# Expert up products: three float32r passes over fixed weight halves, or one full float32 product over weights copied for each slot

## The reference, cut to what matters

```python
# layer 1: gated, no shared expert
g, u = jnp.split(x @ gup.T, 2, axis=-1)              # gup: 1024 x 128 of one expert
acc = acc + ce[:, None] * (jax.nn.silu(g) * u @ dn.T)   # dn: 128 x 512

# layer 2: one up product per expert, and one shared expert for all tokens
shared = jnp.einsum('th,hd->td', jax.nn.silu(x @ shared_w1.T), shared_w2.T)
h = jnp.einsum('td,ehd->teh', x_flat, experts_w1)
expert_out = jnp.einsum('teh,edh->ted', jax.nn.silu(h), experts_w2)
```

## Time and profile before

| what | value |
|---|---|
| median of 3 runs | 3575.4 us (3574.93 to 3579.01) |
| the profiled execution's own time | 3567.43 us |
| its span, first to last instruction | 3565.3 us |
| mean granted TensorE clock | 0.931 of full speed |
| busy: TensorE, VectorE, ScalarE, GpSimd | 3055.0, 2421.9, 2133.5, 1222.4 us |
| first gather to last scatter, layer 2, first run | 2370.83 to 2567.51 us |

### The profile page before, as it was taken

One profiled execution on the slowest core, in us unless ns is written; L12 is line 12 of the kernel. 1 busy time (PEld: TensorE's weight loads), 2 busy tenths in 40 slices (PEclk: granted clock), 3 DMA queues, 4 the chain that ended last, 5 costly groups with the idle time before them and its releaser, 6 DMA issues. The chain is left out here.

```text
span 3565.3 us, 61688 instructions
## 1 busy us (share of the span) xinstructions
PE 3055.0 (86%) x20359; PEld 1919.6 (54%) x20359; DVE 2421.9 (68%) x6667; ACT 2133.5 (60%) x3201; POOL 1222.4 (34%) x1338
## 2 busy tenths in 40 slices
PE   4669999786658967999999779689778987998999
PEld 3533333344447852222222368668756875886787
DVE  7778988576964458999999454454586455656565
ACT  4448989664534545999999735433434344653564
POOL 4454551121546642010010276466536660001000
PEclk9879999998878988999999979899999998999999
DMA  1053440000021122010000321221202122000100
GB/s 58 1 165 112 126 130 18 1 1 24 0 118 40 48 86 89 21 30 21 21 30 2 132 72 48 79 106 46 82 7 93 46 75 80 1 1 10 59 10 12
DMA packets 87166, 187.15 MB, mean 52 GB/s; under 512 B 23169, under 2 KB 41409, under 8 KB 83793
## 3 DMA queue, kind: packets, MB, share of 16 engines
q1 hardware_dynamic: 60048, 117.66, 9.8%
q0 software_dynamic: 26816, 65.58, 5.9%
HBM read 121.23 MB, written 61.34 MB: 51 GB/s over the span
## 5 line engine op out<-in xcount | busy, mean ns | idle before, releaser
L2598 ACT ACTIVATE core_pr<-core_two 128x1024 f32<-128x1024 f32 (+3 forms) x896 | 787.5, 934 | 49.5 <-PE core_two L2565 45.8
L2634 DVE TENSOR_REDUCE core_mx<-core_one 128x1 f32<-128x512 f32 x778 | 491.4, 683 | 20.9 <-PE core_one L2517 13.7
L2577 PE MATMUL core_ps_o<-core_pr,core_vals 128*32 128x512 f32 (+3 forms) x3584 | 434.1, 559 | 1.7 <-ACT core_oT L2609 1.5
L2517 PE MATMUL core_one<-arena,queries 64*128 64x512 bf16 (+3 forms) x1472 | 375.3, 363 | 29.2 <-PEq L62 19.0
L2565 PE MATMUL core_two<-queries,arena 64*128 64x512 bf16 (+3 forms) x1792 | 341.4, 360 | 9.5 <-ACT core_pr L2598 6.8
L2517 PEld LDWEIGHTS core_one<-arena,queries 64*128 64x128 bf16 x1472 | 113.2, 94 | 297.0 <-DVE core_mx L2634 132.2
L2451 POOL COPY core_vals<-arena 128x288 f32<-128x288 f32 x32 | 14.7, 459 | 690.4 <-PE core_ps_o L2577 690.4
L2628 DVE CUSTOM_DVE_ANT_0 core_junk<-core_one,core_over 128x512 bf16<-128x512 f32 (+4 forms) x334 | 201.7, 644 | 26.3 <-PE core_one L2517 21.9
L2565 PEld LDWEIGHTS core_two<-queries,arena 64*128 64x128 bf16 x1792 | 94.3, 94 | 201.7 <-ACT core_pr L2598 145.4
L2604 ACT ACTIVATE core_over<-core_two 128x1024 f32<-128x1024 f32 (+4 forms) x167 | 159.9, 958 | 58.3 <-PE core_two L2540 45.6
L110 DVE CAST moe_second_x_hi<-moe_second_bank 128x128 fp32r<-128x128 f32 x142 | 41.4, 292 | 217.6 <-PE moe_second_bank L573 217.6
(11 more groups left out here) (656 smaller groups left out, 8030.2 us busy)
## 6 DMA issues: line engine op xcount, KB each, us to landing
arena<-expert_out SPq DMA_DIRECT2D x64, 256.0 KB, 3.6
expert_rows<-arena SPq DMA_DIRECT2D x13, 512.0 KB, 8.1
core_w_raw<-in_m_up POOLq DMA_DIRECT2D x25, 256.0 KB, 3.3
m_hi<-core_w_hi POOLq DMA_DIRECT2D x25, 256.0 KB, 2.4
m_lo<-core_w_lo POOLq DMA_DIRECT2D x25, 256.0 KB, 3.0
q_parts<-qkv_parts SPq DMA_DIRECT2D x16, 384.0 KB, 2.6
k_parts<-qkv_parts SPq DMA_DIRECT2D x16, 384.0 KB, 3.4
queries<-q_parts SPq DMA_DIRECT2D x64, 96.0 KB
```

Source lines behind the costliest of these rows:

```text
L2517: pe.matmul(one[bank[e]][:, 0:width], q_sb[rows, hq, pair, qt * P:(qt + 1) * P], k_sb[rows, hq, pair, kc * CW:kc * CW + width], start=True ...
L2577: mm = pe.matmul(ps_o[h * 32:(h + 1) * 32, off:CW], vals[:, hq % 2, j, h, :], pr[:, (n * N2 + k) % KEPT, h // 2, h % 2, off:CW], start=(j ...
L2598: a.activation(pr[:, step % KEPT, i, :, off:CW], two[spot[e] % 2][:, :, off:CW], ACT.Exp, scale=HD ** -0.5).then_inc(s_wide, 1)
L2634: v.tensor_reduce(at, scores, AX.X, ALU.max).then_inc(s_read, 1)
```

## The change

- The up product is a full float32 product with the weights standing and the rows moving: four matmuls of 128x128 for each half of 512, eight for a gated slot, four for a shared one. The result comes out turned, so that `turn_h`, `copy_h` and the tile `h` go; ScalarE's Silu or VectorE's multiply writes `hT` directly, which has 4 places (`HT`) where it had 2.
- [...] VectorE reads the slot's `woff` into a register and copies that expert's 128x512 (gated: 2 x 128x512) from `w_up` to `chosen`, two places in turn. Instead of two instructions that cut the rows it makes one plain copy of them (`copy_x`).
- `psY` has two banks instead of one.
- The float32r halves of the up weights of layers 1 and 2 are no longer made in `core0`, and each sparse stage loads the weights themselves, half as many bytes.
- Shared stages: `gathers_behind` is that of the gated stages, 8 gathers in front and one behind each scatter. The units run on every third round (`EVERY`). CHOOSING is 2 instead of 1. The transposes of chunks 2 and 3 come behind PLACING, those of chunks 4 to 7 into the table rounds 1, 2, 5 and 6; ScalarE normalises groups 2 and 3 behind the first units, group 3 in pieces within the table rounds.

```diff
-    up_hi, up_lo = (st.sb(f"up_{n}", [P, halves * W]) for n in ("hi", "lo"))
+    w_up = st.sb("w_up", [P, halves * W])
...
+    HT = 4
-    fetched = [gathers_behind(s, gated) for s in range(-1, SLOTS)]
+    fetched = [gathers_behind(s) for s in range(-1, SLOTS)]
...
-    CHOOSING, PLACING, ASIDE, BEHIND = (1, 3, 1, 2) if shared else (0, 0, 0, 0)
-    AT = 4
+    CHOOSING, PLACING, ASIDE, BEHIND = (2, 3, 1, 2) if shared else (0, 0, 0, 0)
+    AT, EVERY = 4, 3
+    TURNED_AT = (1, 2, 5, 6)
+    ADDED = {7: 3, 19: 4, 31: 5, 43: 6, 52: 7}
...
             def up(s):
-                pe.wait_ge(s_xlo, s + 1)
+                pe.wait_ge(s_xc, s + 1)
+                pe.wait_ge(s_wc, s + 1)
                 if s >= 2:
                     pe.wait_ge(s_h, s - 1)
                 for half, out in ((0, A), (1, B))[:halves]:
-                    mm = product(pe, out[s % 2][:], (x_hi[:, s % 2, :], x_lo[:, s % 2, :]),
-                                 [t[:, half * W:(half + 1) * W][:, bass.ds(at[s], HID)] for t in (up_hi, up_lo)])
+                    for j in range(4):
+                        mm = pe.matmul(out[s % 2][:, j * P:(j + 1) * P], chosen[:, s % 2, half, j * P:(j + 1) * P],
+                                       xrT[:, s % 2, :], start=True, stop=True)
                     mm.then_inc(s_up if half == halves - 1 else s_gate, 1)
...
-                if 1 <= s <= SLOTS:
-                    turn_h(s - 1)
-                always(1)
+                if s % EVERY == 0:
+                    always(1)
                 if s >= 2:
                     down(s - 2)
...
+            def choose_w(s):
+                e = v.value_load(woff[0:1, s:s + 1], min_val=0, max_val=7 * HID)
+                if s >= 2:
+                    v.wait_ge(s_up, s - 1)
+                v.tensor_copy(chosen[:, s % 2], w_by_half[:, :, bass.ds(e, HID)]).then_inc(s_wc, 1)
+
+            def copy_x(s):
                 v.wait_ge(s_xt, s + 1)
                 if s >= 2:
                     v.wait_ge(s_up, s - 1)
-                upper(v, x_hi[:, s % 2, :], psX[:, 0:P]).then_inc(s_xhi, 1)
-                v.wait_ge(s_xhi, s + 1)
-                lower(v, x_lo[:, s % 2, :], psX[:, 0:P], x_hi[:, s % 2, :]).then_inc(s_xlo, 1)
+                v.tensor_copy(xrT[:, s % 2, :], psX[:, 0:P]).then_inc(s_xc, 1)
...
-        m1_parts, m2_parts, f3_parts = parts("m1", d["m1_up"].shape[1]), parts("m2", d["m2_up"].shape[1]), parts("f3", F3)
+        f3_parts = parts("f3", F3)
```

More of the change, by code:

```diff
@@ L269, with gathers_behind @@
 ROUND = 1.5 * 2.0 ** 23
-def gathers_behind(s, gated):
-    if gated:
-        return min(SLOTS, 8 + s + 1)
-    early = 19
-    if s < early:
-        return min(12 + 2 * (s + 1), s + 24)
-    return min(SLOTS, early + 23 + (s - early + 1) * 2 // 3)
+def gathers_behind(s):
+    return min(SLOTS, 8 + s + 1)
 class Routes:
@@ L294, in __init__, with sparse_stage @@
         self.ones = sb("ones_bf16", [P, P], BF16)
-def sparse_stage(nc, g, name, parts, w_all, w_down, gate_w, gated, lines, room, xrows, ys, loaded, prefetch=None, ahead=0):
+def sparse_stage(nc, g, name, up_all, w_all, w_down, gate_w, gated, lines, room, xrows, ys, loaded, prefetch=None, ahead=0):
     st = Stage(nc, name)
@@ L400, in _ @@
         def _(sp):
[L401 to L404 removed]
+            for f in range(halves):
+                cols = slice(f * W, (f + 1) * W)
+                sp.dma_start(w_up[:, cols], up_all[:, cols]).then_inc(s_wl, 16)
             for i in range(GROUPS_T):
@@ L547, in _ @@
             always(CHOOSING)
-            for c in range(2, 4):
-                turn_xn(c)
             pe.wait_ge(s_chain, TOTAL)
@@ L553, in _ @@
             always(PLACING)
-            for c in range(4, CHUNKS):
+            for c in range(2, 4):
                 turn_xn(c)
@@ L642, in normalise @@
                 a.wait_ge(s_shift, i + 1)
-                for k in range(GT):
+                for k in some:
                     last = a.activation(xn[:, i * GT + k, :], flat(tile_of(g.x, i * GT + k)), ACT.Identity, bias=shift[:, i, k:k + 1],
                                         scale=rstd[:, i, k:k + 1])
-                last.then_inc(s_xn[i], 1)
+                if GT - 1 in some:
+                    last.then_inc(s_xn[i], 1)
             def copy_xn(c):
@@ L669, in _ @@
                 copy_xn(c)
-            for i in range(2, GROUPS_T):
-                normalise(i)
             always(CHOOSING)
+            normalise(2)
+            if not shared:
+                normalise(3)
+            always(PLACING)
             for c in range(2, 4):
                 copy_xn(c)
-            always(PLACING)
-            for c in range(4, CHUNKS):
-                copy_xn(c)
-            always(BEFORE - CHOOSING - PLACING)
+            if shared:
+                for n in range(GROUPS_T * TOPK):
+                    if n in TURNED_AT:
+                        copy_xn(4 + TURNED_AT.index(n))
+                    if n + 1 < GROUPS_T * TOPK:
+                        always(ASIDE)
+                    if n < GT // 2:
+                        normalise(3, range(2 * n, 2 * n + 2))
+            always(BEHIND)
             def active(s):
@@ L706, in _ @@
                     active(s)
-                if gated and 1 <= s <= SLOTS:
-                    copy_h(s - 1)
-                always(1)
+                if s % EVERY == 0:
+                    always(1)
                 if s >= 2:
@@ L838, in multiply @@
                 v.wait_ge(s_up, s + 1)
-                if s >= 2:
-                    v.wait_ge(s_ht, s - 1)
-                v.tensor_tensor(h[:, s % 2, :], silu[:, s % 2, :], B[s % 2][:], ALU.mult).then_inc(s_h, 1)
-            def copy_h(s):
-                v.wait_ge(s_ht, s + 1)
-                if s >= 2:
-                    v.wait_ge(s_down, s - 1)
-                v.tensor_copy(hT[:, s % 2, :], psH[s % 2][:]).then_inc(s_hc, 1)
-            halve_x(0)
-            for s in range(SLOTS + 1):
+                if s >= HT:
+                    v.wait_ge(s_down, s - HT + 1)
+                v.tensor_tensor(hT[:, s % HT, :], silu[:, s % 2, :], B[s % 2][:], ALU.mult).then_inc(s_h, 1)
+            v.wait_ge(s_chain, WOFF)
+            v.wait_ge(s_wl, 16 * halves)
+            choose_w(0)
+            copy_x(0)
+            for s in range(SLOTS):
                 if s + 1 < SLOTS:
-                    halve_x(s + 1)
-                if gated and s < SLOTS:
+                    choose_w(s + 1)
+                    copy_x(s + 1)
+                if gated:
                     multiply(s)
-                if not gated and s >= 1:
-                    copy_h(s - 1)
-                if shared and s in (4, 8, 12, 16, 20):
-                    add(2 + s // 4)
+                if shared and s in ADDED:
+                    add(ADDED[s])
                 if s == 20:
```

78 lines of the change are left out of this document (31 added, 47 removed).

## The result

The changed kernel takes 3525.3 us (median of 4 runs, 3524.5 to 3528.6), the one before 3575.2 (4 runs, 3572.5 to 3579.0): 0.9861 of it, 95% interval 0.9844 to 0.9879, 50 us less. The forecast was 3544 with a range of 3524 to 3582.

What follows compares the result with a forecast made beforehand. Prediction: TensorE bounds every round before; after, TensorE the gated and GpSimd's indirect DMAs the shared loops. Terms -8.6 - 28.8 - 6 - 1 + 13.2 = -31.2 from 3575.4 us give 3544, range 3524 to 3582.

Steps and rivals of the forecast that it cites:

- Gated loops: Both gated slot loops: TensorE's round falls from 2.84 to 2.78 us, 4.3 us a loop, 8.6 for two.
- the fourth rival: TensorE gains less: slower standing products or a 1.21 us weight copy, +7 to +10 a gated loop; 3555 to 3565, chance 0.10.
- Shared loops: Both shared slot loops: GpSimd's 2.56 us pairs set the pace, 182.3 us for 196.7, gaining 14.4 a loop, 28.8 for both.
- f: Share of VectorE's weight copy that delays GpSimd's indirect DMAs in the slot loops; taken as 1/4.
- The copy beside GpSimd: VectorE's weight copy delays GpSimd's indirect DMAs: +6.6 us a shared loop, 0 a gated one, 13.2 in all.
- the first rival: In the slot loops the copy leaves GpSimd untouched, f below 0.1: -44.4 us, 3531; chance 0.33.
- its second case: The forecast itself, slot loops with f between 0.1 and 0.5: 3531 to 3573 us, mostly 3535 to 3555; chance 0.42.
- f = 1: The copy locks GpSimd out in all four loops' indirect DMAs: slower, +54 less core0, 3628 us; chance 0.11.
- Shared routing: Table rounds of both shared stages: round 0 starts earlier after reordering, up to 4 us; 3 a stage taken, 6 in all.
- core0: In core0, 25 of 36 pieces go from GpSimd, so casts wait less: at most 1.2 us, 1 taken.
- the fifth rival: No change: PE's low clock while waiting for GpSimd eats the loops' gains; 3570 to 3580 us, chance 0.04.
- The sum: Whole kernel: -8.6 - 28.8 - 6 - 1 + 13.2 = -31.2 us, giving 3544.

Runs made afterwards that it cites:

- e12: The changed kernel with a shared unit in every round from the first, gathers still 8 ahead, on chip D: 3567.6 us, 0.9986 of the kernel before.
- e7: The changed kernel with the shared loops' weight copy made by ScalarE instead of VectorE, on chip C: 3703.1 us, 1.0048 of the kernel before.
- e8: The changed kernel with the old order of shared units and transposes around the routing tables, on chip C: 3685.8 us, 0.9999 of the kernel before.
- e6: The changed kernel with only every second slot gathered in the shared loops, on chip C: 3602.3 us, 0.9779 of the kernel before.
- e9: The changed kernel with only every second slot gathered in all four loops, on chip D: 3513.9 us, 0.9829 of the kernel before.
- e1: The kernel with new gated stages but the old shared stages, on chip B: 3705.5 us, 1.0061 of the kernel before.
- e10: The kernel before with only every second slot gathered in all four loops, on chip D: 3584.4 us, 1.0032 of the kernel before.

## Why the prediction was right, step by step

- **Gated loops, -4.3 each.** Right. (By the starts in the earlier trace rows the six products with the step take 1.48 and the down product 0.81; the prediction divides the same 2.29 into 1.40 and 0.89, and the rows of after bear out 0.89.) The round is 2.79 for 2.78, and from the first scatter to the last it is 4.4 and 3.5 us less (191.9 for 196.3, 192.0 for 195.5). "The start costs and saves about the same: I count zero" was low: the first scatter comes 1.1 and 2.5 us earlier behind the first gather. Together 5.5 and 6.0. That VectorE keeps up was right, the copy at 0.69; the fourth rival is out.
- **Shared loops, -14.4 each with f = 0.** Right in mechanism: GpSimd sets them. 182.3 was summed, 185.6 and 185.2 came. Of the 3 us about 2.4 are the stretched instructions; the rest is two waits, 1.1 us together, that the sum did not have.
- **The copy beside GpSimd, f = 1/4, +6.6 a loop.** This term was mis-sized, and it was built on the wrong quantity. From the first scatter of the first shared loop on, a scatter and a gather take 0.999 + 0.987 us on the mean; in before, which has no such copy, 0.977 + 0.971. The difference of the sums, 0.038, is 0.09 of the copy's 0.42, so f = 0.09 and 63 x 0.038 = 2.4 us a loop. That lies at the border of the first rival and the forecast: by the prediction's own formula f = 0.1 gives 3536, though it lets its second case begin at 3531. But f is no constant. The same copy gives 0.08 in after's second shared loop, 0.19 and 0.21 in those of e12, and the copy of 0.69 gives 0.14 and 0.13 in the gated loops. What sets it is how often a copy falls on one of the two places of the DMA instruction shown above. That f came out small in after is thus partly luck of the rounds' alignment. L861, on which the prediction leaned, could not tell: it began 0.80 us into its gather, and none of the 34 shared indirect DMAs into which a weight copy began that late got longer either. e7 shows that the stretching is the copy's; that f = 1 is out is shown by after's own trace. Some instructions are long in the gated loops too (25 of 134 over 1.05, at most 1.35), but TensorE's rounds are 2.79 there against pairs of 2.56, so they cost nothing, as said.
- **The Trainium skill** (SBUF — State Buffer, Who interferes with whom) has VectorE and GpSimd lock each other out for the whole instruction. For the copy's instruction the traces agree: all 170 long indirect DMAs of after and e12 end at one of two fixed distances behind the end of a copy. For the indirect DMA's they don't: a copy that begins in its first 0.45 us takes 0.42 to 0.46 like any other, so that 125 of 134 in after's first shared loop are at most 1.05 with a copy in every round, and f is far from 1.
- **Shared routing, -3 each.** Too little: the stretches with the routing are 3.7 and 5.4 shorter. Even the upper end ("up to 4 us") was low for the second. Table round 0 starts when GpSimd has its tiles, as said, and L451 runs through without a wait. The prediction put the lateness of round 0 down to the order alone; it did not see that two of the units in front of it ran at the lower clock (2.8 and 3.0 us), which the new order also ends. e8 shows the order's gain, clock included, as one of its own.
- **core0, -1.** Not shown. The first gather comes 0.9 us earlier, but two executions of before differ by 4.5 us there (1078.9 on A, 1083.4 on D), and after and the runs made from it have 1074.5 to 1080.2.
- **Clock.** 0.99 and 1.00 in the windows though TensorE idles 4% of the shared loop; from 2500 to 2541, where it is busy 34.3 of 41 us, it is 0.96. So the fifth rival is out. (Its "1.00 at 94% busy" is not in the rows shown: the earlier trace rows has 188.4 of 193, 98%.)
- **The sum**, -31.2. With f = 0.09 it would have been -39.6 (2.4 for 6.6 us a loop, 8.4 in all), with the gated loops' 11.5 for 8.6 and the routing's 9.1 for 6 it is -45.6, and the stretches that the change does not touch gave 3.2 back: -42.4, the measured difference of the profiled executions. Against the medians the change is 50: the other 7.5 lie in the profiled execution of before, which I took to stand a fixed 8 us below its median; after's stood 0.5 below. The number is only just inside: 3525.3 lies in the range by 1.3 us, and outside the forecast's own 3533 to 3562. The direction, the bound of either loop and most terms were right; the size was short by 19 us, about 8 by f, 6 by the gated start and the routing, and 7.5 by this execution, less 3 in the stretches that the change does not touch.
- **What the prediction did not price** is what would be left if the pace had not been changed with the products. It said that the early long rounds let GpSimd gather ahead, and it summed the new loop with the new pace, rightly; e12 shows that with gathers 8 ahead the spacing carries 42 of the 50 us, and that without it the shared loops would be longer than before's.

What stays open: the halts of chips B and C, which make every slot loop longer (before's form by 21 us in the gated and by 33 in the shared loops) and leave 7 of the 50 us. That they hang on the indirect DMAs is argued from e6 and not shown: there half the gathers bring a shared loop from 226 to 187 (173 on D). Whether gated loops would recover as well was to be seen in e9, which came to another chip. The packets of these DMAs move in e1 as soon behind their issue as on A (some 1.6 us), so it is not the transfers that are late. The 12 us outside the loops in e9 and e10 stay open too.

## What to carry to other kernels

When products get shorter, sum the engine that feeds them next: half of what TensorE's rounds gained in the shared loops went to GpSimd's indirect DMAs, at 1.28 us each. Work that fills time should be spread so that the slower engine never idles behind a long round and is then itself too slow for the short ones: here that spacing, a change of two lines, was worth 42 us, and without it the shorter products lengthened the shared loops. When one instruction may hold up another, a single row beside it says little: ask where in the other it began. Line up many starts and ends, and look for a fixed distance between the end of one and the end of the other.

## What the runs showed of the hardware

- The same two programs differ by 50 us on chip A and by 7 on chip C, and the kernel before by 3% between chips (3575 and 3573 on A and D, 3683 and 3684 on B and C), each at a mean granted clock of 0.93. At the places looked at, the longer loops have halts of 1.5 to 1.9 us in which ScalarE and VectorE start late on results that TensorE's rows show as done.
- A VectorE copy between SBUF tiles holds up an indirect DMA instruction of 0.97 to 0.99 us only where it covers one of two places in it, about 0.12 us behind its start and 0.12 before its end; there the DMA waits for the end of the copy and ends 0.84 to 0.86 or 0.12 us behind it (170 of 170 long ones in after and e12). It then takes up to 1.24 us beside copies of 0.43, and up to 1.35 beside copies of 0.69. The other way round, copies that begin 0.50 to 0.76 us into it are themselves longer: at most 0.67 for 0.43, and 0.93 for 0.69.
- Behind idle times of 3.7 and 1.2 us TensorE's granted clock was at the lower level (0.59 from 2338 to 2346 of before); a float32 unit took 3.58 us for 1.79.
- 16 records of 128x128 float32 products with a new standing tile each take 1.79 us, the same 0.11 a record whether the standing tile is a weight or rows of activations.
